# Four graph layers on one core: the last stage's weights and the split of their products made in the graph layer, flags and rows turned by transposes, the first unit's projection split by VectorE

## The chip, the cores and the metric

The kernel runs on one core of a Trainium2 chip. A core has TensorE (PE, with its weight loads shown apart as PEld), VectorE (DVE), ScalarE (ACT), GpSimd (POOL), and SyncE (SP), which here issues the DMA transfers. The metric is the time of one execution on the device in microseconds, as the median of several runs; lower is better.

## The reference

Four residual layers over x of shape [8, 1024, 64] (batch, node, feature) with one adjacency matrix adj [1024, 1024] of zeros and ones. Before each there is a layer norm and a relu:

```python
h = maximum(layernorm(x), 0); x = x + hypergraph_layer(h, ...)      # L0
h = maximum(layernorm(x), 0); x = x + graph_attention(h, adj, ...)  # L1
h = maximum(layernorm(x), 0); x = x + graph_layer(h, adj, ...)      # L2
h = maximum(layernorm(x), 0); x = x + last_attention(h, adj, ...)   # L3

def graph_layer(x, A, weights):          # two rounds
    for i in range(2):
        x = relu(einsum('bmf,fg->bmg', einsum('mn,bnf->bmf', A, x), weights[i]))

def gat_layer(x, graph, W, b):           # used by last_attention
    h = x @ W                            # per head 64 -> 128; at the end 1024 -> 64
    s = einsum('bnd,bmd->bnm', h, h) * graph
    s = where(s == 0.0, -1e16, s)
    return einsum('bnm,bmd->bnd', softmax(s, axis=2), h) + b

def last_attention(x):                   # 8 heads, then one more attention over their outputs
    heads = [gat_layer(x, graph, Wh[i], bh[i]) for i in range(8)]
    x = leaky_relu(concat(heads), 0.01)
    return leaky_relu(gat_layer(x, graph, W_out, b_out), 0.01)
```

## The kernel before

The four layers run one after the other as four stages; x, h and the adjacency stay on the core between them. The change touches the third stage (graph layer, function `graph_layer`) and the fourth (`last_attention`).

**The graph layer** goes through quarters of two batches: rows are turned, projected with a weight (L880 for the second), parted into a rounded high and a low float32r half, and multiplied with the adjacency. The second product, L905, is the last large one; behind each of its eight tiles DVE adds x (L1065) and the layer norm for the next stage follows. At its end the stage makes what the next one needs of rows that are all zero: flags `gl_zero` [128, 8] for each of eight tiles become the rows `marks` [8, 1024] by eight fp32 matmuls against the identity (L939), and counts [8, 1024] become columns by eight more (L945). DVE's L1139 makes `row_scale` of them.

**The last stage** works in units. A head unit is one batch and one head; there are 64, in order of batches, and then eight output units, one per batch. As h W Wᵀ hᵀ is wanted, the kernel forms the gram matrix W Wᵀ of each head once (W stacked twice, so 128 x 128), splits it into high and low halves, and projects y = gram · rows (`project`, L303). Of a unit:

- PE's `project` writes y for unit g+2; ACT rounds it to `y_hi` (`round_y`, L519) and copies it to `y_wide` (`copy_y`, L526); POOL subtracts and adds the marks, giving `y_lo` (`split_y`, L637 and L639).
- For each of eight tiles of 128 rows PE makes four matmuls of 512 columns (`score`, L318: rows `hid_xs` against y high and low), DVE masks the tile with the adjacency and takes the row maximum (`mask_tile`, L450), ACT takes the exponential (L535), DVE transposes the tile in 32 x 32 blocks (`turn_tile`, L459). Scores run two tiles ahead of DVE, in two PSUM buffers.
- Four parts of 32 small matmuls (`values`, L338) then sum the values of the unit before, and `head_out`, `project_out` carry it on.

The rows `hid_xs` of a batch are its h turned by `turn_rows(n, part, bank)`: for each of four tiles two fp32 matmuls of h (128 x 64) against the identity, one written to PSUM partitions 0 to 63, one to 64 to 127 (L282). ACT rounds them (`round_rows`, L512), DVE subtracts in the upper half (`split_rows`, L421), so that the upper half holds the low part. For batches 1 to 7 the two parts are turned behind tile 6 of the units 3 and 4 of the batch before (units are counted from 0), between that tile's scores and `project_out`. Output units call `turn_rows` for both parts in `project`.

**Order.** No planner is at work: each engine's program is the order written in the loops over g and t, and engines wait for each other by counting semaphores. At the start of the last stage the order on PE is: turn both parts for batch 0, wait for the weights, eight gram matmuls (in each round ACT takes the high half, DVE the low half, L484, before PSUM is free again), `project(0)`, `project(1)`, `score(0)`. On SP: the marks to DRAM (L230), six weight loads (L232), x saved to DRAM (L233), the marks read back to all partitions (L227), then the rows that `values` wants. The weights land in `weights_t`, a buffer that the first `turn_tile` overwrites later. L43 is a line of the start of a stage's block.

Of the kernel before, what the change touches and what calls it, by code (L numbers as in the profile page):

```python
# [5 lines left out]
ALU = mybir.AluOpType  # L6
# [6 lines left out]
P = 128  # L13
B, N, F = 8, 1024, 64
NT = N // P
# [34 lines left out]
def split(nc, ctx, name, shape):  # L50

    return (ctx.enter_context(nc.sbuf_tensor(name + "_hi", shape, F32R)),
            ctx.enter_context(nc.sbuf_tensor(name + "_lo", shape, F32R)))


def last_attention(nc, m, w, d, x_saved):
# [9 lines left out]
    with ExitStack() as ctx:  # L66
# [6 lines left out]
        wh_t, wz, wo, bias, weights_t = w.wh_t, w.wz, w.wo, w.bias, w.weights_t  # L73
        gram = split(nc, ctx, name + "_gram", [P, HEADS, P])
# [30 lines left out]
        gram_ready = sem("gram_ready")  # L105
        gram_hi = sem("gram_hi")
        gram_split = sem("gram_split")
# [3 lines left out]
        weights_loaded = sem("weights_loaded")  # L111
# [66 lines left out]
        def _(sp):  # L178
# [52 lines left out]
            for place, src in w.loads:  # L231
                sp.dma_start(place, src).then_inc(weights_loaded, 16)  # L232
# [44 lines left out]
        def _(pe):  # L277
            def turn_rows(n, part, bank):
                for k in range(4):
                    t = 4 * part + k  # L280
                    for c in range(2):
                        ins = pe.matmul(m.ps_low[c * F:(c + 1) * F, bank, k * P:(k + 1) * P],  # L282
                                        m.h[:, t, n, :], m.ident[:], start=True, stop=True)
                return ins
# [132 lines left out]
        def _(dve):  # L417
# [91 lines left out]
        def _(act):  # L509
# [2103 lines left out]
```

## Time and profile before

| | us |
|---|---|
| median of 3 runs | 2303.24 (2299.11 to 2304.76) |
| profiled execution, its own time | 2298.83 |
| span in the profile | 2296.8 |
| PE busy | 2048.7 (89%) |
| DVE busy | 2022.9 (88%) |
| ACT busy | 1406.3 (61%) |
| POOL busy | 950.3 (41%) |
| PEld busy | 1352.5 (59%) |

The profile is of one execution. The span is the time from the first to the last recorded instruction; the execution's own time is 2.0 us longer. Busy shares are means over four stages that work differently: the last stage begins at 742 us and has two thirds of the span. In a timeline row the number ahead is the start in us, the next the length; an "x32" joins 32 records of one kind, and the bracket gives the idle time of the engine just before and what ended it. fp32 matmuls have two records each.

### The profile page before, as it was taken

How to read it: one execution, taken by the hardware profiler on the slowest of the kernel's cores; microseconds unless marked ns; L12 is line 12 of the kernel's file. 1: busy time of each engine (PE TensorE's matmuls, PEld its weight loads, DVE VectorE, ACT ScalarE, POOL GpSimd, SP SyncE). 2: the span in 40 equal slices, each digit the busy share in tenths (PEclk: the TensorE clock that was granted, in tenths of full speed). 3: DMA queues.
4: the chain of work that ended last, by engine and by line, in shares of the span. 5: the costliest groups of instructions: out<-in, count | busy, mean ns of one | idle time of the engine just before them, and what ended most of it. 6: DMA issues, size and time to landing. Idle time of an engine off the chain costs nothing. (4 is left out here: it accounts for less than half of the span.)

```text
span 2296.8 us, 61374 instructions
## 1 busy us (share of the span) xinstructions
PE 2048.7 (89%) x26446; PEld 1352.5 (59%) x26446; DVE 2022.9 (88%) x2704; ACT 1406.3 (61%) x2186; POOL 950.3 (41%) x542
## 2 busy tenths in 40 slices
PE   5888867478688699999999999999999999998886
PEld 5654436345476466666666666666666666665555
DVE  7568857499657699999999999999999999999995
ACT  4422225499631467666777666776667676676774
POOL 2259972136400244444444344444444444432211
PEclk9999977578988799999999999999999999999998
DMA  3000000534200320021111211201210210123442
GB/s 127 1 0 0 0 1 1 93 65 67 38 2 11 92 53 30 29 57 39 41 42 33 53 34 39 53 25 39 52 43 30 57 30 30 34 58 65 71 66 47
DMA packets 176817, 94.72 MB, mean 41 GB/s; under 512 B 158552, under 2 KB 163864, under 8 KB 176432
## 3 DMA queue, kind: packets, MB, share of 16 engines
q1 hardware_dynamic: 176560, 90.94, 18.0%
q8 instruction: 204, 3.34, 0.6%
q14 instruction: 53, 0.43, 0.1%
HBM read 80.09 MB, written 10.83 MB: 40 GB/s over the span
## 5 line engine op out<-in xcount | busy, mean ns | idle before, releaser
L535 ACT ACTIVATE x_sb<-x_sb,hid_neg_max 128x1024 f32<-128x1024 f32 x576 | 661.6, 1154 | 289.6 <-DVE hid_neg_max L450 289.4
L459 DVE STREAM_TRANSPOSE hid_weights_t<-x_sb 128x1024 f32<-128x1024 f32 x576 | 709.2, 1231 | 1.6 <-ACT x_sb L535 1.2
L450 DVE CUSTOM_DVE_ANT_0 x_sb<-ps_score,adj_mask,row_scale 128x1024 f32<-128x1024 f32 x512 | 636.1, 1242 | 16.2 <-PE ps_score L318 15.0
L338 PE MATMUL ps_low<-hid_weights_t,hid_x_rep 32*64 32x256 f32 x18432 | 577.5, 384 | 11.1 <-ACT hid_share L565 10.7
L318 PE MATMUL ps_score<-hid_y_hi,hid_xs 128*128 128x512 f32 x1152 | 522.7, 454 | 33.0 <-DVE hid_neg_max L450 27.4
L338 PEld LDWEIGHTS ps_low<-hid_weights_t,hid_x_rep 32*64 32x64 f32 x18432 | 393.2, 132 | 169.4 <-issue 98.0
L318 PE MATMUL ps_score<-hid_y_lo,hid_xs 128*128 128x512 f32 x1152 | 457.1, 397 | 0.0
L645 POOL TENSOR_TENSOR hid_z<-hid_z,hid_inv_cols 128x1024 f32<-128x1024 f32 x64 | 194.1, 3032 | 554.6 <-ACT hid_z L543 554.6
L318 PEld LDWEIGHTS ps_score<-hid_y_hi,hid_xs 128*128 128x128 f32 x1152 | 217.6, 189 | 259.7 <-issue 155.2
L318 PEld LDWEIGHTS ps_score<-hid_y_lo,hid_xs 128*128 128x128 f32 x1152 | 218.9, 190 | 44.2 <-issue 15.0
L637 POOL TENSOR_TENSOR hid_y_wide<-hid_y_wide,hid_y_hi 128x1024 f32<-128x1024 f32 x64 | 153.5, 2398 | 192.0 <-ACT hid_y_wide L526 192.0
L639 POOL TENSOR_TENSOR hid_y_lo<-hid_y_wide,marks 128x1024 fp32r<-128x1024 f32 x64 | 152.9, 2389 | 5.0
L350 PE MATMUL ps_low<-hid_z,hid_wz 128*128 128x512 f32 x256 | 121.8, 598 | 4.4 <-DVE hid_xs L421 3.9
L535 ACT ACTIVATION_READ_ACCUMULATOR x_sb<-x_sb,hid_neg_max 128x1 f32 x576 | 112.1, 195 | 0.0
L543 ACT COPY hid_z<-ps_low 128x1024 f32<-128x1024 f32 x72 | 73.1, 1016 | 47.7 <-PE ps_low L338 47.7
L2157 POOL TENSOR_TENSOR h_sb<-h_sb,hyp_share 128x512 f32<-128x512 f32 x72 | 94.9, 1318 | 5.7
L519 ACT CAST hid_y_hi<-ps_low 128x1024 fp32r<-128x1024 f32 x72 | 73.1, 1015 | 29.0 <-PE ps_low L303 16.5
L1397 ACT ACTIVATE ps_score<-gat_e_wide,e 128x1024 f32<-128x1024 f32 x64 | 70.8, 1107 | 25.0 <-PE ps_score L1272 19.1
L578 ACT COPY hid_share<-ps_low 128x512 f32<-128x512 f32 x56 | 32.9, 588 | 81.9 <-PE ps_low L366 81.9
L656 POOL TENSOR_TENSOR h_sb<-h_sb,hid_share 128x512 f32<-128x512 f32 x56 | 74.5, 1330 | 17.2 <-ACT hid_share L578 17.2
L2139 ACT ACTIVATE hyp_blend_exp<-ps_score,hyp_minus_one 128x512 f32<-128x512 f32 x54 | 37.1, 688 | 71.3 <-PE ps_score L2120 71.3
L450 DVE CUSTOM_DVE_ANT_0 x_sb<-ps_score,hid_masks,hid_row_flag 128x1024 f32<-128x1024 f32 x64 | 79.3, 1239 | 0.0
(349 smaller groups left out, 3059.9 us busy)
## 6 DMA issues: line engine op xcount, KB each, us to landing
hid_inv_cols<-hid_inv_rows SPq DMA_DIRECT2D x64, 512.0 KB, 3.7
hid_x_rep<-hid_row_space SPq DMA_DIRECT2D x64, 256.0 KB, 5.7
gat_x_rep<-gat_row_space SPq DMA_DIRECT2D x32, 256.0 KB, 5.7
gat_e_wide<-gat_e_space SPq DMA_DIRECT2D x8, 512.0 KB, 6.4
marks<-hid_mark_rows SPq DMA_DIRECT2D x8, 512.0 KB, 5.0
x_sb<-in_x SPq DMA_DIRECT2D x4, 512.0 KB, 6.0
hyp_neighbours<-in_adj SPq DMA_DIRECT2D x4, 512.0 KB, 7.2
edge_adj_high<-in_adj SPq DMA_DIRECT2D x4, 512.0 KB, 8.9
```

The costliest lines, as they stand in the source:

```text
L318: ins = pe.matmul(m.ps_score[:, i % 2, half * HALF:(half + 1) * HALF], xs[:, batch_of(g) % 2, t * P:(t + 1) * P], y[g % 2][k][:, half * HA ...
L338: ins = pe.matmul(m.ps_low[c * F:(c + 1) * F, a, 0:NT * Q], x_rep[a * Q:(a + 1) * Q, batch_of(g) % 2, b, :], weights_t[a * Q:(a + 1) * Q, ...
L350: ins = pe.matmul(m.ps_low[:, half, :], wz[:, g % HEADS, :], z[:, half * HALF:(half + 1) * HALF], start=True, stop=True)
L450: dve.tensor_tensor_reduce(ring[:, i % RING, :], m.ps_score[:, i % 2, :], mask, scale, HUGE, ALU.add, ALU.min, neg_max[:, g % 2, t:t + 1]) ...
L459: dve.transpose(weights_t[:, g % 2, :, t, :], ring[:, i % RING, :].rearrange("p (b j) -> p b j", j=Q)).then_inc(tile_turned, 1)
L519: act.copy(y[g % 2][0][:], wide(y_banks(g))).then_inc(y_hi, 1)
L535: act.activation(ring[:, i % RING, :], ring[:, i % RING, :], ACT.Exp, scale=-1.0, bias=neg_max[:, g % 2, t:t + 1], accum_out=row_sum[:, g ...
L637: pool.tensor_tensor(y_wide[:], y_wide[:], y[g % 2][0][:], ALU.subtract).then_inc(y_lo, 1)
L639: pool.tensor_tensor(y[g % 2][1][:], y_wide[:], m.marks[:], ALU.add).then_inc(y_split, 1)
L645: pool.tensor_tensor(rows, rows, inv_cols[:].rearrange("p i t -> p t i"), ALU.mult)\
L656: pool.tensor_tensor(out, out, share[:].rearrange("p (t f) -> p t f", f=F), ALU.add)\
L2157: pool.tensor_tensor(rows[:, t, :], rows[:, t, :], s, ALU.add)\
```

## The change

- `last_weights` is called ahead of `graph_layer`; the six weight loads are issued on SP in the graph layer, behind that layer's own four. `wh_t` and the gram get buffers of their own, on the other side of SBUF ("right").
- The eight gram matmuls stand in the graph layer as `square_weights`, between the last projection and the second product, into one PSUM bank pair; ACT copies the high half and DVE takes the low half in one instruction each.
- Flags and counts are turned by `pe.transpose` in place of matmuls with the identity.
- In `turn_rows` the lower half is made by `pe.transpose`, the upper half stays a matmul. Output units and head units use the same function.
- The first unit's `copy_y` (ACT) and `split_y` (POOL, two operations) are gone; DVE makes both from PSUM, behind `split_rows`.

```diff
@@ last_attention, SP
             sp.dma_start(mark_rows, m.marks[0:B, :]).then_inc(marks_stored, 16)
-            for place, src in w.loads:
-                sp.dma_start(place, src).then_inc(weights_loaded, 16)
             sp.dma_start(x_saved, m.x[:].rearrange("p t b f -> p (t b f)")).then_inc(x_copied, 16)
@@ last_attention, PE
             def turn_rows(n, part, bank):
                 for k in range(4):
                     t = 4 * part + k
-                    for c in range(2):
-                        ins = pe.matmul(m.ps_low[c * F:(c + 1) * F, bank, k * P:(k + 1) * P],
-                                        m.h[:, t, n, :], m.ident[:], start=True, stop=True)
+                    pe.transpose(m.ps_low[0:F, bank, k * P:(k + 1) * P], m.h[:, t, n, :], m.ident[:])
+                    ins = pe.matmul(m.ps_low[F:P, bank, k * P:(k + 1) * P], m.h[:, t, n, :], m.ident[:],
+                                    start=True, stop=True)
                 return ins
...
             for part in range(2):
                 turn_rows(0, part, prep_bank(0, part)).then_inc(x_turned, 1)
-            pe.wait_ge(weights_loaded, 16 * len(w.loads))
             pe.wait_ge(x_split, 2)
-            for h in range(HEADS):
-                if h > 1:
-                    pe.wait_ge(gram_split, h - 1)
-                w2 = wh_t[:, h, :, :].rearrange("p a f -> p (a f)")
-                pe.matmul(m.ps_low[:, h % 2, 0:P], w2, w2, start=True, stop=True).then_inc(gram_ready, 1)
-            pe.wait_ge(gram_split, HEADS)
             project(0)
@@ last_attention, DVE
             split_rows(0, 1)
-            for h in range(HEADS):
-                dve.wait_ge(gram_hi, h + 1)
-                dve.tensor_tensor(gram[1][:, h, :], m.ps_low[:, h % 2, 0:P], gram[0][:, h, :],
-                                  ALU.subtract).then_inc(gram_split, 1)
+            dve.wait_ge(y_hi, 1)
+            dve.tensor_tensor(y_wide[:], wide(y_banks(0)), y[0][0][:], ALU.subtract).then_inc(y_copied, 1)
+            dve.wait_ge(y_copied, 1)
+            dve.wait_ge(marks_loaded, 16)
+            dve.tensor_tensor(y[0][1][:], y_wide[:], m.marks[:], ALU.add).then_inc(y_split, 1)
             dve.wait_ge(x_copied, 16)
@@ last_attention, ACT
-            for h in range(HEADS):
-                act.wait_ge(gram_ready, h + 1)
-                act.copy(gram[0][:, h, :], m.ps_low[:, h % 2, 0:P]).then_inc(gram_hi, 1)
             round_y(0)
-            copy_y(0)
             round_y(1)
@@ last_attention, POOL
-            split_y(0)
@@ graph_layer, SP
+            for place, src in last.loads:
+                sp.dma_start(place, src).then_inc(last_loaded, 16)
@@ graph_layer, PE
+            def square_weights():
+                pe.wait_ge(last_loaded, 16 * len(last.loads))
+                pe.wait_ge(parted[0], 2 * QB)
+                for h in range(HEADS):
+                    w2 = last.wh_t[:, h, :, :].rearrange("p a f -> p (a f)")
+                    ins = pe.matmul(m.ps_score[:, 1, h * P:(h + 1) * P], w2, w2, start=True, stop=True)
+                ins.then_inc(gram_ready, 1)
...
             project_second(QB - 1)
+            square_weights()
...
             pe.wait_ge(flags_ready, 1)
+            pe.wait_ge(gram_split, 1)
             for t in range(NT):
-                ins = pe.matmul(m.ps_score[0:B, 1, t * P:(t + 1) * P], zero[:, t, :], m.ident[:],
-                                start=True, stop=True)
+                ins = pe.transpose(m.ps_score[0:B, 1, t * P:(t + 1) * P], zero[:, t, :], m.ident[:])
...
             for t in range(NT):
-                ins = pe.matmul(m.ps_low[:, 0, t * B:(t + 1) * B], counts[:, t * P:(t + 1) * P],
-                                m.ident[0:B, 0:B], start=True, stop=True)
+                ins = pe.transpose(m.ps_low[:, 0, t * B:(t + 1) * B], counts[:, t * P:(t + 1) * P],
+                                   m.ident[0:B, 0:B])
@@ graph_layer, ACT, behind the last round_second
+            act.wait_ge(gram_ready, 1)
+            act.copy(last.gram[0][:].rearrange("p h c -> p (h c)"), m.ps_score[:, 1, :]).then_inc(gram_hi, 1)
@@ graph_layer, DVE, behind the last part_second
+            dve.wait_ge(gram_hi, 1)
+            gram_lo = last.gram[1][:].rearrange("p h c -> p (h c)")
+            dve.tensor_tensor(gram_lo, m.ps_score[:, 1, :], last.gram[0][:].rearrange("p h c -> p (h c)"),
+                              ALU.subtract).then_inc(gram_split, 1)
```

PE's order at the start of the last stage, from the counts' last matmuls to the first projection. `h_sb` are the rows to be turned. Before:

```order
L945 MATMUL ps_low<-ident,gl_counts 128x8 x8
L782 UNCONDITIONAL_BRANCH
L276 UNCONDITIONAL_BRANCH
L282 MATMUL ps_low<-ident,h_sb 64x128 x16
L379 MATMUL ps_low<-hid_weights_t 128x128 x8
L303 MATMUL ps_low<-hid_xs,hid_gram_hi 128x512
```

After, where L275 is the transpose and L276 the matmul (the pair stands eight times):

```order
L940 MATMUL ps_low<-ident,gl_counts 128x8 x8
L764 UNCONDITIONAL_BRANCH
L270 UNCONDITIONAL_BRANCH
L275 MATMUL ps_low<-ident,h_sb 64x128
L276 MATMUL ps_low<-ident,h_sb 64x128
L275 MATMUL ps_low<-ident,h_sb 64x128
L276 MATMUL ps_low<-ident,h_sb 64x128
```

The same sixteen instructions turn the rows, now of two kinds in turn, and the eight gram matmuls between them and the projection are gone.

They stand in the graph layer now, between the last projection and the second product. PE there, before:

```order
L880 MATMUL ps_score<-gl_w,gl_bent 128x128 x16
L905 MATMUL ps_low<-gl_second_hi,adj_t_sb 128x512
L905 MATMUL ps_low<-gl_second_lo,adj_t_sb 128x512
L905 MATMUL ps_low<-gl_second_hi,adj_t_sb 128x512
```

After:

```order
L874 MATMUL ps_score<-gl_w,gl_bent 128x128 x16
L841 MATMUL ps_score<-hid_wh_t 128x128 x8
L899 MATMUL ps_low<-gl_second_hi,adj_t_sb 128x512
L899 MATMUL ps_low<-gl_second_lo,adj_t_sb 128x512
```

The second product starts behind eight instructions more.

DVE's order at the start of the last stage, from the last operation of the graph layer to the first mask (written ISA). Before:

```order
L1139 SCALAR_TENSOR_TENSOR row_scale<-ps_low,gl_sign 128x64
L782 UNCONDITIONAL_BRANCH
L416 UNCONDITIONAL_BRANCH
L421 TENSOR_TENSOR hid_xs<-ps_low,hid_xs 64x512 x2
L484 TENSOR_TENSOR hid_gram_lo<-ps_low,hid_gram_hi 128x128 x8
L450 ISA x_sb,hid_neg_max<-ps_score,adj_mask,row_scale 128x1024
```

After:

```order
L1140 SCALAR_TENSOR_TENSOR row_scale<-ps_low,gl_sign 128x64
L764 UNCONDITIONAL_BRANCH
L403 UNCONDITIONAL_BRANCH
L408 TENSOR_TENSOR hid_xs<-ps_low,hid_xs 64x512 x2
L470 TENSOR_TENSOR hid_y_wide<-ps_low,hid_y_hi 128x1024
L473 TENSOR_TENSOR hid_y_lo<-hid_y_wide,marks 128x1024
L437 ISA x_sb,hid_neg_max<-ps_score,adj_mask,row_scale 128x1024
```

Eight small subtractions are replaced by two operations of 1024 columns, the second of which reads the marks.

## Rows read from the trace of the kernel before

**Rows 1.** Stretch, its length, busy PE, PEld, DVE, ACT, POOL, clock, DMA share, GB/s
```profile
742.40:769.10 26.70, 14.54 (x61) 11.30 (x62) 3.72 (x10) 7.42 (x14) 5.00 (x3) 0.56 0.90 200
769.10:2063.00 1293.90, 1274.80 (x19264) 822.01 (x19271) 1286.82 (x1678) 896.82 (x1358) 577.35 (x263) 1.00 0.16 40
2063.00:2296.80 233.80, 189.30 (x2980) 130.76 (x2962) 208.67 (x258) 158.07 (x311) 49.99 (x31) 0.92 0.36 61
```

**Rows 2.** Timeline (start, length, engine, line, operation, idle before), start of last stage
```profile
742.44 3.68 PE L282 MATMUL ps_low<-ident,h_sb 128*64 128x128 f32 x32 [1.16 <-PEq L43]
...
746.16 0.59 ACT L512 CAST hid_xs<-ps_low 128x512 fp32r<-128x512 f32 x1 [1.12 <-PE ps_low L282]
...
746.78 0.69 DVE L421 TENSOR_TENSOR hid_xs<-ps_low,hid_xs 64x512 fp32r<-64x512 f32 x1 [1.01 <-ACT hid_xs L512]
748.06 0.43 SPq L233 DMA_DIRECT2D x_saved<-x_sb  x1
...
751.66 1.22 PE L379 MATMUL ps_low<-hid_weights_t 128*128 128x128 f32 x4 [5.53 <-DMA hid_bias<-in_bh_t]
...
757.99 0.79 PE L303 MATMUL ps_low<-hid_xs,hid_gram_hi 128*128 128x512 f32 x1 [0.68 <-DVE hid_gram_lo L484]
...
760.10 1.01 ACT L519 CAST hid_y_hi<-ps_low 128x1024 fp32r<-128x1024 f32 x1 [2.49 <-PE ps_low L303]
...
766.92 0.79 PE L318 MATMUL ps_score<-hid_y_hi,hid_xs 128*128 128x512 f32 x1 [5.15 <-POOL hid_y_lo L639]
...
769.15 1.28 DVE L450 CUSTOM_DVE_ANT_0 x_sb<-ps_score,adj_mask,row_scale 128x1024 f32<-128x1024 f32 x1 [11.21 <-PE ps_score L318]
```

**Rows 3.** DMA issue there: count, KB, us from issue to landing
```profile
marks<-hid_mark_rows SPq DMA_DIRECT2D x1, 512.0 KB, 10.6
```

**Rows 4.** Timeline, PE between the last projection and the second product
```profile
690.25 2.02 PE L880 MATMUL ps_score<-gl_w,gl_bent 128*128 128x128 f32 x16 [1.45 <-issue]
...
692.78 0.50 PE L905 MATMUL ps_low<-gl_second_hi,adj_t_sb 128*128 128x512 f32 x1 [0.51 <-DVE gl_second_lo L1052]
```

**Rows 5.** Timeline, DVE at the second product's second tile
```profile
700.39 0.69 DVE L1065 SCALAR_TENSOR_TENSOR x_sb<-ps_low,x_sb 128x512 f32<-128x512 f32 x1 [0.36 <-PE ps_low L905]
```

**Rows 6.** Timeline of the end of the graph layer
```profile
734.19 3.58 PE L939 MATMUL ps_score<-ident,gl_zero 128*8 128x128 f32 x16 [0.71 <-DVE gl_zero L1132]
...
737.70 3.58 PE L945 MATMUL ps_low<-ident,gl_counts 8*128 8x8 f32 x16
...
741.32 0.23 DVE L1139 SCALAR_TENSOR_TENSOR row_scale<-ps_low,gl_sign 128x64 f32<-128x64 f32 x1 [2.30 <-PE ps_low L945]
```

**Rows 7.** Timeline, PE around one output unit's turned rows
```profile
2092.67 0.40 PE L318 MATMUL ps_score<-hid_y_hi,hid_xs 128*128 128x512 f32 x1
2092.91 0.40 PE L318 MATMUL ps_score<-hid_y_lo,hid_xs 128*128 128x512 f32 x1
2093.23 1.97 PE L282 MATMUL ps_low<-ident,h_sb 128*64 128x128 f32 x32
2095.13 0.50 PE L318 MATMUL ps_score<-hid_y_hi,hid_xs 128*128 128x512 f32 x1
2095.47 0.40 PE L318 MATMUL ps_score<-hid_y_lo,hid_xs 128*128 128x512 f32 x1
```

**Rows 8.** The weight loads of these turned rows
```profile
2093.23 1.73 PEld L282 LDWEIGHTS ps_low<-ident,h_sb 128*64 128x64 f32 x32 [0.37 <-issue]
```

**Rows 9.** Timeline, PE and PEld: eight transposes, 64 columns wide
```profile
95.71 1.00 PEld L1971 LDWEIGHTS ps_score<-ident,table_elus 128*64 128x64 f32 x8
...
95.94 1.04 PE L1971 MATMUL ps_score<-ident,table_elus 128*64 128x128 f32 x8
...
96.90 0.29 PEld L1975 LDWEIGHTS ps_score<-hyp_rank,hyp_upper 64*128 64x128 f32 x2 [0.20 <-issue]
```

**Rows 10.** Timeline, DVE behind a head unit's turned rows
```profile
1031.46 1.28 DVE L450 CUSTOM_DVE_ANT_0 x_sb<-ps_score,adj_mask,row_scale 128x1024 f32<-128x1024 f32 x1 [0.23 <-PE ps_score L318]
```

**Rows 11.** DVE's waits, last stage to 2063: us in total, times, longest
```profile
DVE x_sb L450 <- PE ps_score L318: 15.0, 17, 11.2
```

More of the change, by code:

```diff
@@ L47, with split @@
     pass
-def split(nc, ctx, name, shape):
-    return (ctx.enter_context(nc.sbuf_tensor(name + "_hi", shape, F32R)),
-            ctx.enter_context(nc.sbuf_tensor(name + "_lo", shape, F32R)))
+def split(nc, ctx, name, shape, side="left"):
+    return (ctx.enter_context(nc.sbuf_tensor(name + "_hi", shape, F32R, side=side)),
+            ctx.enter_context(nc.sbuf_tensor(name + "_lo", shape, F32R, side=side)))
 def last_attention(nc, m, w, d, x_saved):
@@ L71, in sem @@
             return nc.alloc_semaphore(f"{name}_{n}")
-        wh_t, wz, wo, bias, weights_t = w.wh_t, w.wz, w.wo, w.bias, w.weights_t
-        gram = split(nc, ctx, name + "_gram", [P, HEADS, P])
+        wz, wo, bias, gram = w.wz, w.wo, w.bias, w.gram
+        weights_t = sb("weights_t", [P, 2, NB, NT, Q])
         ring = m.x[:].rearrange("p (r t) b f -> p r (t b f)", r=RING)
@@ L103, in last_attention @@
         col_rows = nc.dram_tensor("hid_col_rows", (B, P, NT), BF16).ap()
-        gram_ready = sem("gram_ready")
-        gram_hi = sem("gram_hi")
-        gram_split = sem("gram_split")
         x_copied = sem("x_copied")
@@ L110, in last_attention @@
         out_rows_loaded = sem("out_rows_loaded")
-        weights_loaded = sem("weights_loaded")
         rows_saved = sem("rows_saved")
@@ L637, in split_y @@
                 pool.tensor_tensor(y_wide[:], y_wide[:], y[g % 2][0][:], ALU.subtract).then_inc(y_lo, 1)
-                pool.wait_ge(y_lo, g + 1)
+                pool.wait_ge(y_lo, g)
                 pool.tensor_tensor(y[g % 2][1][:], y_wide[:], m.marks[:], ALU.add).then_inc(y_split, 1)
@@ L700, with __init__ @@
 class Weights:
-    def __init__(self, nc, ctx, name):
-        self.nc, self.ctx, self.name, self.clear, self.loads = nc, ctx, name, [], []
+    def __init__(self, nc, ctx, name, side="left"):
+        self.nc, self.ctx, self.name, self.clear, self.loads, self.side = nc, ctx, name, [], [], side
     def buffer(self, n, shape):
-        return self.ctx.enter_context(self.nc.sbuf_tensor(f"{self.name}_{n}", shape, F32))
+        return self.ctx.enter_context(self.nc.sbuf_tensor(f"{self.name}_{n}", shape, F32, side=self.side))
     def load(self, place, src):
@@ L758, in graph_weights, with last_weights @@
     return g
-def last_weights(nc, ctx, d):
-    g = Weights(nc, ctx, "hid")
-    g.weights_t = g.buffer("weights_t", [P, 2, N // 32, NT, 32])
-    g.wh_t = g.weights_t[:, 0, 0:4, :, :].rearrange("p a (h k) i -> p (a h) (k i)", k=4)\
-        .rearrange("p h (k f) -> p h k f", k=2)
+def last_weights(nc, ctx, own, d):
+    g = Weights(nc, ctx, "hid", "right")
+    g.wh_t = own.enter_context(nc.sbuf_tensor("hid_wh_t", [P, HEADS, 2, F], F32))
+    g.gram = split(nc, ctx, "hid_gram", [P, HEADS, P], "right")
     g.wz = g.buffer("wz", [P, HEADS, HID])
@@ L774, in last_weights, with graph_layer @@
     return g
-def graph_layer(nc, m, g):
+def graph_layer(nc, m, g, last):
     QB = B // 2
@@ L810, in graph_layer @@
         mixed, mix_bent = sem("mixed"), sem("mix_bent")
+        last_loaded, gram_ready, gram_hi, gram_split = (
+            sem("last_loaded"), sem("gram_ready"), sem("gram_hi"), sem("gram_split"))
         summed, x_added = sem("summed"), sem("x_added")
@@ L2564, in four_layers @@
             with fresh_semaphores(nc), ExitStack() as own:
-                graph_layer(nc, m, graph_weights(nc, own, d))
-        with fresh_semaphores(nc), ExitStack() as own:
-            g = last_weights(nc, own, d)
+                g = last_weights(nc, ctx, own, d)
+                graph_layer(nc, m, graph_weights(nc, own, d), g)
+        with fresh_semaphores(nc):
             x_saved = nc.dram_tensor("x_saved", (P, NT * B * F), F32).ap()
```

## The prediction

> **What bounds the kernel now.** Read the page first for the shares: DVE is busy 88% and PE 89% of the span. That is an average, so read the busy time by stage next [rows 1]. In the 64 head units (769.1 to 2063) DVE is busy 1286.8 of 1293.9 us, PE 1274.8: DVE sets the pace and PE stands just behind. The waits say how close: DVE waited for a score tile 17 times, 15.0 us in all, and 11.2 of that is the one wait before its first tile [rows 11, 2]. So 16 small waits, 3.8 us, are left, and the timeline shows where they sit, for example 0.23 us right behind a unit's turned rows [rows 10]. I counted them in DVE's timeline: nearly all follow a turn of rows. Whatever lengthens PE there is paid by DVE; in units without a turn PE has a few tenths to spare.
>
> The other place is the start of the last stage, 742.4 to 769.1, where DVE works 3.7 of 26.7 us [rows 1]. Read it as a chain in the timeline [rows 2]: rows turned on PE from 742.44, taken by ACT at 746.16 and by DVE until 747.47, then PE idle for the last weight transfer until 751.66, eight rounds of PE, ACT and DVE for the gram until 757.99, projection until 760.10, rounding on ACT, two subtractions and additions on POOL, first scores at 766.92, DVE's first tile at 769.15.
>
> **The change, part by part.** All times are of the profiled execution (span 2296.8, its own time 2298.83 us); the median of the runs is 2303.24. I carry differences over to the median.
>
> *Flags and counts by transposes.* Each of the 16 fp32 matmuls there is two records: 16 records from 734.19 to 737.70, and 16 more, 3.58 us, to the end at 741.32 [rows 6]. A transpose is one record per tile: eight of them pass in 1.04 us elsewhere in the kernel [rows 9], (1.04 - 0.27)/7 = 0.11 us each, 0.27 being the last one's own length. So half the records go: 3.51/2 + 3.58/2, less a little tail, is 3.4 us gained. Between nothing (a transpose as long as two records) and 3.5. On the path, since DVE's last operation waits for it. The marks' DVE operation fits beside the counts' transposes.
>
> *Gram in the graph layer.* Eight matmuls, 16 records like those of the projection before them. That projection starts at 690.25 and its slots are over at about 690.25 + 2.02 - 0.16 = 692.1; 16 more at 0.11 make 1.75, so the second product starts at 693.9 instead of 692.78 [rows 4]: 1.1 us late. DVE is the slower engine in that product but starts on PE's tiles, and waits 0.36 us for the second [rows 5], so all of it is paid. ACT's copy (1.01, as the rounding in rows 2) and DVE's subtraction (1.28, as L450 there) fall into the idle stretch before DVE's first tile at about 697.9: 693.9 + 0.3 + 1.0 + 1.3 = 696.5. Nothing. Bounds for the matmuls: 0.6 (partly beside the wait that is there) to 2.9 (at the half clock). The weights' six transfers run over 60 us before they are used.
>
> So the last stage starts 3.4 - 1.1 = 2.3 us sooner, at about 740.1.
>
> *Start of the last stage.* The wait for weights and the gram rounds are gone. POOL's two operations become two of DVE, 1.28 each. From the end of the turning to DVE's first tile: 746.16 to 747.47 (1.31), 0.1, projection 757.99 to 760.10 (2.11), rounding 1.01, DVE 2 x 1.28, small hand-overs 0.1, then 766.92 to 769.15 (2.23): 9.4 us. What is late next: the marks, which the second DVE operation needs. They landed 748.54 + 10.6 = 759.1, that is 11.1 us behind the issue of x_saved, their predecessor in the queue [rows 2, 3]. x_saved is now issued behind one small transfer at 740.4, so the marks are there at 751.5 at the latest, earlier by up to 2 us since no weights are ahead. Were turning as long as before (3.72 us), DVE would be ready for the marks at 740.1 + 3.72 + 9.4 - 2.23 - 1.28 = 749.7, would wait for them, and the first tile would stand at 755.0: 14.2 us gained, 15.9 without the wait.
>
> *Turned rows: the term that goes the other way.* Per tile two matmuls of 64 columns turn the same rows into the lower and the upper 64 partitions. Now they run side by side: 32 records take 1.90 us from 2093.23 to 2095.13, 0.22 us per pair of matmuls less the switch, where two records one behind the other take 0.22 by themselves [rows 7]. The lower one becomes a transpose. Three rows speak on whether it still shares the array. The scores before the turned rows pass every 0.24 us (2092.67, 2092.91), but the first turned row starts 0.32 behind, its weights loaded only then, PEld idle 0.37 [rows 7, 8]: entering the side-by-side form costs 0.09, with its exposed load 0.14. Leaving it costs 0.09, and the next record follows at 0.34 instead of 0.24: another 0.10, for 128 columns of weights; for 64 I take half. The 64-column transposes there are [rows 9] behave otherwise: their first weights load while the full-width matmul streams and no gap opens, and the matmul after them waits, PEld idle 0.20. So a transpose of this form looks like an operation of the full array, and alternating with a half-width matmul means two switches per tile. Per tile: transpose 0.11, into it 0.14, matmul 0.22, into that 0.14: 0.61 against 0.22. A part of four tiles: 0.11 + 4 x 0.36 + 3 x 0.25 = 2.3 against 0.14 + 0.88 = 1.0, 1.3 us more. Bounds: nothing (side by side as before) to 1.8 (if each switch also bares the 128-column load).
> The Trainium skill says the same from the other side: the page TensorEngine Tiling (Array Packing), Restrictions and Gotchas, Gotcha 2, has column tiling and transposes of fp32 exclude each other on trn2. No row here shows the two alternate. By the rule the sum is the one below; without it the first rival's.
>
> Seven batches turn two parts each inside head units, and there PE's lateness is DVE's wait [rows 10]: 14 x 1.3 = 18.2, less about 0.07 each where PE still had something in hand: 17.2 us lost. At the start of the stage, at the half clock (0.56 over that stretch [rows 1]), a pair takes 3.72/8 = 0.46; records double, switches perhaps not: 0.9 to 1.2 per tile, eight tiles, 3.5 to 6 us more, I take 4.5. The marks hide 1.8 of it: 14.2 becomes 11.5. In the last eight units eight tiles are turned per unit, 2.7 us more on PE, but PE is busy 189.3 of 233.8 us there [rows 1] and DVE's tiles take longer than PE's; I take 0.5 in all.
>
> Sum: -11.5 + 17.2 + 0.5 = +6.2 us. Profiled 2305.0; as a median 2309.4. About 0.3% (6.9 us) is what a measurement of this kernel tells from no change, so this is the edge of it, 0.27%. The case itself spans +1 to +13.
>
> **Rivals.** *The transpose shares the array.* Then only the start counts: -14.2 to -15.9, 2288. For it: the two matmuls share today. Against: the loads that hide [rows 9]. The Trainium skill's page Perfetto Trace Analysis, section Transposes, asks for transposes in place of matmuls, as cheaper; the trace agrees [rows 9] for a run of them alone.
> *One behind the other, without switches.* 0.11 per tile more, 0.43 per part: 14 x 0.43 - 0.9 = 5.1; at the start 1.7, hidden by the marks. -14.2 + 5.1 = -9.1: 2294. Against it: both switches in rows 7.
> *Slower: the cover in the last eight units fails.* The turning stands between two score tiles: 2.7 us more make it 4.6, with the tiles' scores 6.5, while DVE has two tiles in hand, about 5.2. Each of eight units loses 1.3, 10 us more: 2320. It decides once PE's burst is longer than DVE's two tiles. Against: PE idles a fifth of that stretch.
>
> **How the numbers follow.** Main case 0.5; shared array 0.1; one behind the other 0.2; failed cover 0.13; the rest (marks or clock otherwise) 0.07. Faster by over 0.3% is the shared case, most of the serial one and little else: 0.28. Within: a bit over half of the main case and edges: 0.34. Slower: 0.38. Range: leave out the shared case and the far end: 2291 to 2319. The main case by itself: 2304 to 2316.
>
> **What would show it.** The stage's first DVE tile near 757.6 (755 if transposes share); transposes and matmuls of the turned rows starting 0.2 to 0.4 us apart in turn, not together; a part of 2.3 us; DVE waits of 1.3 to 1.5 us in the fourth and fifth unit of every batch, some 20 us in all; L905 1.1 us later; the flags' two groups half as long. I am wrong if a part still takes 1.0 us, or if DVE does not wait behind it.

## The result and the profile after

The changed kernel takes 2317.69 us in the median (2316.77 to 2318.48, 4 runs), the kernel before 2302.25 (2299.11 to 2304.76, 4 runs with those shown above): a ratio of 1.0069, 95% interval 1.0057 to 1.0081. It is 15.4 us slower. The forecast was 2309.4: the direction is the forecast one, but two terms of the sum were too small. The measured time lies inside the stated range (2291 to 2319) and outside the main case's (2304 to 2316).

The profiled execution has a span of 2315.0 us, 18.2 more than before. Not all of it belongs to the change. The first two stages are the same code in both, and yet DVE's first reduction of the graph layer stands at 633.14 instead of 629.49; over all profiled kernels it lay between 628.5 and 637.2. So I count from that instruction:

| us | before | after |
|---|---|---|
| graph layer, to `row_scale` | 111.8 | 108.8 |
| to the last stage's first tile on DVE | 139.7 | 127.1 |
| from there to the end of the first unit | 24.8 | 25.7 |
| 56 units more | 1137.8 | 1156.9 |
| 8 units more | 173.3 | 174.0 |
| rest (the last seven output units and what follows them) | 191.9 | 198.2 |
| from the graph layer to the end | 1667.4 | 1681.9 |

(A unit's end is DVE's reciprocal of its row sums, one row per unit in the timeline. The 56 units hold all fourteen turned parts of head units; the eight behind them are seven head units and the first output unit.) Three terms stand out: -12.6 at the start, +19.2 in the head units, +6.3 in the output units.

The same windows by stage as in [rows 1], of after:

```profile
743.02:760.21 17.19, 13.84 (x37) 7.65 (x38) 3.84 (x5) 4.48 (x5) 0.32 (x1) 0.50 0.96 230
760.21:2078.00 1317.79, 1300.04 (x19218) 830.26 (x19217) 1288.45 (x1678) 897.60 (x1359) 577.86 (x263) 1.00 0.16 40
2078.00:2315.00 237.00, 201.55 (x2892) 133.33 (x2890) 198.91 (x257) 157.14 (x309) 50.66 (x31) 0.93 0.36 60
```

In the head units DVE is as busy as before (1288.5 against 1286.8 us), while the 56 units of the table are 19.2 us longer. DVE's waits say why; of after, from the first tile to 2078 (us in total, times, longest), to be laid beside [rows 11]:

```profile
DVE x_sb L437 <- PE ps_score L312: 29.1, 26, 2.8
```

Of these, 2.3 are the wait of the first tile, which in [rows 11] was 11.2. So where there were 16 small waits with 3.8 us there are 25 now with 26.8. Fourteen of them stand one each behind the fourteen turned parts of the head units; they last 1.43 to 1.61 us each, 21.3 in all. The timeline of PE and DVE there, of after, where L275 is the transpose and L276 the matmul:

```profile
858.58 0.40 PE L312 MATMUL ps_score<-hid_y_lo,hid_xs 128*128 128x512 f32 x1
859.02 0.30 PE L275 MATMUL ps_low<-ident,h_sb 128*64 128x128 f32 x1
859.25 0.43 PE L276 MATMUL ps_low<-ident,h_sb 128*64 128x128 f32 x2
859.62 0.30 PE L275 MATMUL ps_low<-ident,h_sb 128*64 128x128 f32 x1
859.85 0.43 PE L276 MATMUL ps_low<-ident,h_sb 128*64 128x128 f32 x2
...
862.25 0.50 PE L312 MATMUL ps_score<-hid_y_hi,hid_xs 128*128 128x512 f32 x1
...
863.49 1.28 DVE L437 CUSTOM_DVE_ANT_0 x_sb<-ps_score,adj_mask,row_scale 128x1024 f32<-128x1024 f32 x1 [1.61 <-PE ps_score L312]
```

A pair starts every 0.60 us: 0.23 from the transpose to the matmul, 0.37 from the matmul with its two records to the next transpose. The forecast had 0.61 (0.25 and 0.36). DVE waits 1.61 us behind it, where before it waited 0.23 behind such a part [rows 10].

The start of the last stage, of after, beside [rows 2]:

```profile
743.05 0.40 PE L275 MATMUL ps_low<-ident,h_sb 128*64 128x128 f32 x1 [1.36 <-PEq L43]
...
750.19 0.69 PE L276 MATMUL ps_low<-ident,h_sb 128*64 128x128 f32 x2
750.92 0.59 ACT L500 CAST hid_xs<-ps_low 128x512 fp32r<-128x512 f32 x1 [3.31 <-PE ps_low L276]
...
752.28 0.80 PE L297 MATMUL ps_low<-hid_xs,hid_gram_hi 128*128 128x512 f32 x1 [1.40 <-DVE hid_xs L408]
...
755.44 1.22 DVE L470 TENSOR_TENSOR hid_y_wide<-ps_low,hid_y_hi 128x1024 f32<-128x1024 f32 x1 [3.21 <-ACT hid_y_hi L507]
...
756.70 1.22 DVE L473 TENSOR_TENSOR hid_y_lo<-hid_y_wide,marks 128x1024 fp32r<-128x1024 f32 x1
...
760.21 1.28 DVE L437 CUSTOM_DVE_ANT_0 x_sb<-ps_score,adj_mask,row_scale 128x1024 f32<-128x1024 f32 x1 [2.28 <-PE ps_score L312]
```

Turning takes 7.8 us instead of 3.7, and still the stage's first tile comes 17.2 us behind its first turned row instead of 26.7. The wait for weights and the rounds of the gram are gone, and no wait for the marks is seen: they had landed (issued 744.91, 7.4 us) when DVE came to them.

The flags, and the gram in the graph layer, of after:

```profile
695.77 1.95 PE L841 MATMUL ps_score<-hid_wh_t 128*128 128x128 f32 x16
...
697.48 0.47 PE L899 MATMUL ps_low<-gl_second_hi,adj_t_sb 128*128 128x512 f32 x1
...
738.88 1.87 PE L935 MATMUL ps_score<-ident,gl_zero 128*8 128x128 f32 x8 [0.71 <-DVE gl_zero L1133]
...
740.68 1.02 PE L940 MATMUL ps_low<-ident,gl_counts 8*128 8x8 f32 x8
...
741.93 0.20 DVE L1140 SCALAR_TENSOR_TENSOR row_scale<-ps_low,gl_sign 128x64 f32<-128x64 f32 x1
```

The second product starts 64.3 us into the graph layer (697.48 - 633.14) instead of 63.3 (692.78 - 629.49, [rows 4]): 1.05 us for the gram. The two groups of [rows 6] take 1.87 and 1.02 us instead of 3.58 each.

In the output units another engine shows the cost. ACT around the turned rows of an output unit, of after (L507 rounds them, L523 is the exponential), and DVE's next block transpose:

```profile
2135.97 1.02 ACT L507 CAST hid_y_hi<-ps_low 128x1024 fp32r<-128x1024 f32 x1 [4.22 <-PE ps_low L276]
...
2137.79 1.15 ACT L523 ACTIVATE x_sb<-x_sb,hid_neg_max 128x1024 f32<-128x1024 f32 x1
...
2142.98 1.19 ACT L523 ACTIVATE x_sb<-x_sb,hid_neg_max 128x1024 f32<-128x1024 f32 x1
...
2144.30 1.25 DVE L446 STREAM_TRANSPOSE hid_weights_t<-x_sb 128x1024 f32<-128x1024 f32 x1 [1.83 <-ACT x_sb L523]
```

The tile whose mask was over at 2132.3 could have had its exponential at once. It got it at 2137.79: ACT's program has the rounding of the turned rows ahead of it, and ACT stood waiting for them for 4.22 us. The work that piled up on ACT also made the next tile's exponential late (2142.98), and that is the one DVE waits for. Over the stretch ACT's waits for them were, of before and then of after:

```profile
ACT hid_y_hi L519 <- PE ps_low L282: 11.2, 7, 1.9
```

```profile
ACT hid_y_hi L507 <- PE ps_low L276: 30.0, 7, 4.6
```

DVE, which before had no wait for scores or exponentials over 0.15 us from 2063 on, has 13.6 us of them from 2078 on in after: 8.6 for exponentials, 5.0 for scores. The loss of 6.3 us in the table's rest is less than half of that, because something else got shorter at the same time: 25 of DVE's mask operations (L435 before, L422 after) stand in that stretch, and they take 37.8 us before and 30.8 after. The last section shows what they depend on.

### The profile page after: what moved, and what is told of

Read it like the earlier page. It is cut to its first block and busy times, and to the rows that moved or that the text cites. A ratio compares the mean times of both kernels' runs of the same rounds, so it can differ in the third digit from the quotient of the medians.

```text
span 2315.0 us, 61072 instructions
## 1 busy us (share of the span) xinstructions
PE 2089.7 (90%) x26302; PEld 1364.1 (59%) x26302; DVE 2016.4 (87%) x2699; ACT 1404.2 (61%) x2178; POOL 946.7 (41%) x540
## 5 line engine op out<-in xcount | busy, mean ns | idle before, releaser
L523 ACT ACTIVATE x_sb<-x_sb,hid_neg_max 128x1024 f32<-128x1024 f32 x576 | 661.5, 1153 | 266.7 <-DVE hid_neg_max L437 266.5
L523 ACT ACTIVATION_READ_ACCUMULATOR x_sb<-x_sb,hid_neg_max 128x1 f32 x576 | 112.0, 195 | 0.0
L507 ACT CAST hid_y_hi<-ps_low 128x1024 fp32r<-128x1024 f32 x72 | 73.1, 1015 | 54.0 <-PE ps_low L276 34.0
```

The lines of the kernel that those rows point to most:

```text
L507: act.copy(y[g % 2][0][:], wide(y_banks(g))).then_inc(y_hi, 1)
L523: act.activation(ring[:, i % RING, :], ring[:, i % RING, :], ACT.Exp, scale=-1.0, bias=neg_max[:, g % 2, t:t + 1], accum_out=row_sum[:, g ...
```

## Experiments

One theory and its rivals were left after the two traces. *A*: the loss is the alternation of a transpose with a half-width matmul, in the head units by PE alone, in the output units by way of ACT's order. The rivals: the loss has another source (buffers moved to the other side of SBUF, or PE's idle time at the start gone), or needs the rest of the change; and for the output units, PE's burst alone starves DVE. All times of stages are counted as in the table above: first tile / 56 units / rest / all from the graph layer on.

| | median us | ratio to before | first tile | 56 units | rest | all |
|---|---|---|---|---|---|---|
| before | | 1 | 139.7 | 1137.8 | 191.9 | 1667.4 |
| after | 2317.7 | 1.0069 (1.0057 to 1.0081) | 127.1 | 1156.9 | 198.2 | 1681.9 |
| turn_matmul | 2287.4 | 0.9929 (0.9910 to 0.9948) | 123.2 | 1138.3 | 193.2 | 1653.4 |
| before_turned | 2326.9 | 1.0106 (1.0086 to 1.0126) | 139.9 | 1156.5 | 199.0 | 1694.9 |
| turn_grouped | 2293.5 | 0.9962 (0.9946 to 0.9977) | 122.2 | 1146.0 | 191.0 | 1657.6 |
| act_order | 2305.8 | 1.0029 (1.0020 to 1.0038) | 126.2 | 1156.9 | 190.0 | 1671.2 |
| act_order_matmul | 2278.5 | 0.9899 (0.9884 to 0.9914) | 122.1 | 1138.1 | 188.6 | 1644.5 |
| flags_matmul | 2288.8 | 0.9943 (0.9928 to 0.9958) | 126.4 | 1138.2 | 193.2 | 1656.7 |
| pool_split | 2291.2 | 0.9954 (0.9939 to 0.9969) | 126.2 | 1138.3 | 191.8 | 1654.5 |
| best | 2280.6 | 0.9903 (0.9887 to 0.9920) | 121.9 | 1138.2 | 188.6 | 1645.1 |
| marks_first | 2282.8 (1 run) | | 121.9 | 1138.2 | 191.8 | 1650.0 |
| gram_late | 2287.8 (1 run) | | 127.1 | 1138.1 | 192.3 | 1655.9 |

The kernel before, run beside each group: 2301.3 (turn_matmul to turn_grouped), 2299.6 (act_order to pool_split), 2303.9 (the last three). Where a stage is compared to a us, the traces decide, since the two stages ahead move the whole by several us from one execution to the next. But each trace is one execution too. Kernels with the same code up to that point differ in the first tile by 1.1 us (turn_matmul 123.2, act_order_matmul 122.1) and by 0.9 (after 127.1, act_order 126.2); those with the same output units differ in the rest by 1.4 (191.8 to 193.2). The 56 units repeat to 0.2 (1138.1 to 1138.3). A difference of about 1 us outside the 56 units is therefore not shown by one pair of traces.

**turn_matmul**: undo one part.

```diff
-                    pe.transpose(m.ps_low[0:F, bank, k * P:(k + 1) * P], m.h[:, t, n, :], m.ident[:])
-                    ins = pe.matmul(m.ps_low[F:P, bank, k * P:(k + 1) * P], m.h[:, t, n, :], m.ident[:],
-                                    start=True, stop=True)
+                    for c in range(2):
+                        ins = pe.matmul(m.ps_low[c * F:(c + 1) * F, bank, k * P:(k + 1) * P],
+                                        m.h[:, t, n, :], m.ident[:], start=True, stop=True)
```

> The changed kernel, but all rows are turned by the two half-width matmuls again. Theory (the transposes of turned rows cost; all other parts of the change gain): the fourteen turned parts in head units give back 14 x 1.37 = 19 us, the output units some 7, the start of the last stage 4 (turning 3.7 us instead of 7.8), in all about -30 against the changed kernel: 2288, and about 15 us faster than the kernel before. Rival (the loss has another cause, as the buffers moved to the other side of SBUF or the missing idle time): at most 10 us come back, 2308 or more.

2287.4 us, faster than before by 0.7%. The 56 units are back at 1138.3, the first tile comes 3.9 us sooner, the rest is 5.0 shorter. The loss is the turned rows'; the rival falls. At the start the shorter turning (4.1 us) is not the only thing that moved. DVE now waits 1.2 us for the marks, while the projection runs faster: from its first matmul to ACT's rounding it takes 1.24 us here, at a granted clock of 1.00, against 2.12 us in after, at 0.50.

**before_turned**: the same three lines the other way round, in the kernel before.

> The kernel before, with the lower half of every turned row made by a transpose and nothing else changed. Theory: +19 us in the head units, +7 in the output units, nothing at the start (PE waits for the last weights until 751.7 there, and the turning, 7.8 us instead of 3.7, is over by then): 2302 + 26 = 2328. Rival (the loss needs the other parts of the change): under +10, 2312 or less. On the output units alone: if the loss there is from ACT waiting for the rows, it is +5 to +9 here too; if it is an accident of how masks and GpSimd met, it is between 0 and +14.

2326.9: +18.7 in the 56 units, +7.1 in the rest, +0.2 at the first tile. The loss needs nothing else of the change, and at the start the weights hid it.

**turn_grouped**: the switch against the load.

```diff
                 for k in range(4):
                     t = 4 * part + k
                     pe.transpose(m.ps_low[0:F, bank, k * P:(k + 1) * P], m.h[:, t, n, :], m.ident[:])
+                for k in range(4):
+                    t = 4 * part + k
                     ins = pe.matmul(m.ps_low[F:P, bank, k * P:(k + 1) * P], m.h[:, t, n, :], m.ident[:],
```

> The changed kernel, but of each part first the four transposes and then the four half-width matmuls. The pairs now start every 0.60 us. Theory A (each switch between a transpose and a half-width matmul costs 0.12 to 0.14): only two switches are left of eight, a part takes 4 x 0.11 + 0.13 + 4 x 0.22 + 0.13 = 1.6 us instead of 2.3: 0.75 x 14 = 10 us less in the head units, 4 in the output units, 3 at the start (half clock): 2300. Theory B (every load of 64 columns is bare, whatever the record ahead was): a part still takes 2.3 us, the time stays within 2 us of 2317.7. Theory C (the transposes then hide beside the matmuls): 2290 or less.

The 56 units gain 10.9 us, as theory A had it; the start gains 4.9 and the rest 7.1, more than was put down. At the start the expectation reckoned with the half clock, and 0.66 was granted over this run's turning (747 to 752), 0.50 over that of after (743 to 751). B is out, and C too, since 8 us are still missing against two matmuls. A part in turn_grouped (L275 transposes, L278 matmuls, L362 the output projection):

```profile
834.73 0.63 PE L275 MATMUL ps_low<-ident,h_sb 128*64 128x128 f32 x4
835.28 0.76 PE L278 MATMUL ps_low<-ident,h_sb 128*64 128x128 f32 x5
835.78 0.64 PE L362 MATMUL ps_low<-hid_hidden,hid_wo 128*64 128x512 f32 x1
835.88 0.49 PE L278 MATMUL ps_low<-ident,h_sb 128*64 128x128 f32 x3
...
837.16 0.50 PE L314 MATMUL ps_score<-hid_y_hi,hid_xs 128*128 128x512 f32 x1
```

Four transposes pass in 0.55 us with one switch behind them. The first matmul of the output projection, which goes to the other half, starts while the last matmuls of the upper half still come: half-width matmuls share, and here the transposes did not. In turn_matmul the sharing is plain, since the records of the two halves start in twos, the first at 854.53 and 854.54 and from the second two on a new one about every 0.11 us:

```profile
854.53 1.09 PE L276 MATMUL ps_low<-ident,h_sb 128*64 128x128 f32 x16
855.46 1.03 PE L360 MATMUL ps_low<-hid_hidden,hid_wo 128*64 128x512 f32 x4
856.42 0.50 PE L312 MATMUL ps_score<-hid_y_hi,hid_xs 128*128 128x512 f32 x1
```

From the first turned row to the next score: 1.89 us here, 2.43 in groups, 3.23 in turn, the same for all fourteen parts of each run. The differences to turn_matmul, 1.34 in turn and 0.54 in groups, times 14 parts are 18.8 and 7.6; the 56 units lost 18.6 and 7.7 against turn_matmul.

**act_order**: the changed kernel, ScalarE's order alone.

```diff
                     if g < UNITS:
                         exp_tile(g * NT + t)
+                    if t == 0 and HEAD_UNITS <= g + 1 < UNITS:
+                        round_y(g + 1)
...
-                    if t == 7 and g + 2 < UNITS:
+                    if t == 7 and g + 2 < HEAD_UNITS:
                         round_y(g + 2)
```

> The changed kernel, but for output units ScalarE rounds the turned rows (round_y) behind the next unit's first exponential instead of ahead of it. In the changed kernel ScalarE waits 30.0 us there in seven waits (11.2 before), with that exponential queued behind it. Theory (the output units lose their 6 to 7 us because ScalarE's queue stands behind the longer turning): DVE's waits for the exponential there, 8.6 us in all, go, and the part behind the 65th unit's start takes 190 to 193 us instead of 198.2; the whole 2317.7 - 6 = 2312. Rival (PE's burst of 4.7 us starves DVE of scores by itself): it stays at 197 or more, 2317.

The rest falls from 198.2 to 190.0 us with PE's burst as long as before. ACT waits 17.3 us for the rows instead of 30.0, and DVE's waits from 2077 on, of act_order, are:

```profile
DVE hid_weights_t L446 <- ACT x_sb L523: 5.0, 5, 1.1
DVE x_sb L437 <- PE ps_score L312: 1.3, 2, 0.7
```

They were 8.6 and 5.0 in after. The mask operations of the rest take the same time in both (30.9 and 30.8 us), so the 8.2 us are mostly these 7.3 us of waits. The theory named the size of the gain, but not its parts: the waits for exponentials were to go, and 5.0 us of them stay, while the waits for scores, which it did not name, fell by 3.7. So ACT's order makes somewhat more than half of what DVE waits in the output units, and the rival, a burst of PE that starves DVE by itself, is wrong for most of it. The cause of the 6.3 us that stay is not separated. Only part of the 11.9 us between the medians is the edit's: in the traces 1.8 us of the gain stand at the first tile and in the first unit, which it does not touch.

**act_order_matmul**: both edits together.

> The same move on ScalarE, with all rows turned by matmuls. There ScalarE waits only about 11 us for the rows. Theory: DVE is busy 90% of the output units there, so little is left to gain: 1 to 3 us less than with the matmuls alone, 2285. Rival (ScalarE's later rounding delays the next unit's rows): 0 to 4 us more, 2290.

2278.5 us, 1.0% faster than before, the lowest of all. The move gains more than I put down: 4.6 us in the rest and 2.4 in the eight units ahead of it (170.7 instead of 173.1), against turn_matmul. But not by way of DVE's waits for exponentials, of which there were none to speak of in turn_matmul's output units. The traces show where it comes from. In the rest the mask operations are 2.8 us shorter (34.7 instead of 37.5), and the stretch behind DVE's last instruction is 1.8 shorter (24.5 instead of 26.3), a stretch that took 24.9 to 26.3 in the five kernels with turn_matmul's output units, so this part may be chance. In the eight units ahead the masks are 1.4 shorter and DVE's small waits 1.0. One such mask operation beside GpSimd's, of turn_matmul and then of act_order_matmul:

```profile
2139.60 2.37 POOL L616 TENSOR_TENSOR hid_y_lo<-hid_y_wide,hid_y_hi 128x1024 fp32r<-128x1024 f32 x1 [19.07 <-ACT hid_y_wide L514]
2140.42 2.63 DVE L422 TENSOR_TENSOR hid_masks<-adj_mask,hid_col_mask 128x2048 bf16<-128x2048 bf16 x1
```

```profile
2133.92 2.38 POOL L618 TENSOR_TENSOR hid_y_lo<-hid_y_wide,hid_y_hi 128x1024 fp32r<-128x1024 f32 x1 [18.22 <-ACT hid_y_wide L514]
2135.56 1.81 DVE L422 TENSOR_TENSOR hid_masks<-adj_mask,hid_col_mask 128x2048 bf16<-128x2048 bf16 x1
```

The new order lets ACT's copy, and with it GpSimd's operation, come 0.8 us sooner against the mask, which then has less of it to sit out. It is so in five of the last six units with such a meeting; in one (2161.12) the mask starts 0.4 us behind GpSimd and takes 3.09 us.

**flags_matmul**: on turn_matmul, `pe.transpose` of flags and counts back to `pe.matmul` with start and stop.

> Rows turned by matmuls, and flags and counts turned by matmuls too. Counted from the start of the graph layer, row_scale is made at +108.8 us with transposes. Theory (16 records less, 3.1 us between the kernels and 1.05 for the gram that came in): +112.9, the first tile of the last stage 4.1 later, and the time 2287.4 + 4 = 2291.5. Rival (a transpose is paid like two records; the gain is from elsewhere): within 1 us of 108.8.

`row_scale` at +111.5, so the transposes gain 2.7, and 3.2 at the first tile. It is less than 4.1 because the counts' matmuls had the higher clock in this run (0.65 granted over 737 to 743, where before had 0.50 over both groups):

```profile
737.17 3.58 PE L935 MATMUL ps_score<-ident,gl_zero 128*8 128x128 f32 x16 [0.71 <-DVE gl_zero L1134]
...
740.68 2.18 PE L941 MATMUL ps_low<-ident,gl_counts 8*128 8x8 f32 x16
```

The first group takes 3.58 as in [rows 6], the second 2.18 instead of 3.58. What raised the clock here and not before stays open. The medians do not separate this kernel from turn_matmul (1.4 us apart, intervals that overlap).

**pool_split**: on turn_matmul, DVE's two operations out, `copy_y(0)` and `split_y(0)` back.

> Rows turned by matmuls, and the first unit's y split by ScalarE's copy and GpSimd again. Theory: from the end of the rounding to the first score 5.8 us as before, against 3.8 now of which 1.2 is a wait for the marks: the first tile 2.0 us later, 2289.4. Rival (the marks or DVE's place in the chain hide it): less than 0.5 us.

The first tile is 3.0 us later, not 2.0. POOL waits for the marks ahead of its first operation, where DVE waits only ahead of its second; so on POOL both operations stand behind the marks:

```profile
756.13 2.34 POOL L617 TENSOR_TENSOR hid_y_wide<-hid_y_wide,hid_y_hi 128x1024 f32<-128x1024 f32 x1 [9.31 <-DMA marks<-hid_mark_rows]
758.54 2.34 POOL L619 TENSOR_TENSOR hid_y_lo<-hid_y_wide,marks 128x1024 fp32r<-128x1024 f32 x1
```

So the 3.0 us are the price of this order as much as of the engine. The medians are 3.8 us apart in the same direction, with intervals that overlap.

**marks_first** and **best**: the marks' transfer ahead of the saving of x, on turn_matmul and on act_order_matmul.

```diff
-            sp.dma_start(x_saved, m.x[:].rearrange("p t b f -> p (t b f)")).then_inc(x_copied, 16)
             sp.wait_ge(marks_stored, 16)
             load_marks(0)
+            sp.dma_start(x_saved, m.x[:].rearrange("p t b f -> p (t b f)")).then_inc(x_copied, 16)
```

> Rows turned by matmuls, and the marks read back ahead of the saving of x; ScalarE's order as in the changed kernel. Theory as for the kernel before this one: first tile at +122.0 instead of +123.2. Rival: +124 to +125, a wait for the saved x ahead of the first tile.

> Rows turned by matmuls, ScalarE's rounding behind the next exponential in output units, and the marks read back ahead of the saving of x. With the rows turned by matmuls the first unit's second DVE operation waits 1.2 us for the marks. Theory (their transfer stands behind the 2 MB of x): it lands 2 to 4 us sooner, the first tile stands at +121 us from the start of the graph layer instead of +122.1 to +123.2, and the time is about 2277.5. Rival (DVE's first tile then waits for x to be saved, which is issued 2 us later and takes 7.5): +123 or more, 2280.

The marks land in 4.3 us instead of 7.8, and their wait, 1.18 us in turn_matmul, is gone. Another takes its place; DVE's first tile in turn_matmul and in marks_first:

```profile
757.07 1.28 DVE L437 CUSTOM_DVE_ANT_0 x_sb<-ps_score,adj_mask,row_scale 128x1024 f32<-128x1024 f32 x1 [2.28 <-PE ps_score L312]
```

```profile
753.04 1.28 DVE L437 CUSTOM_DVE_ANT_0 x_sb<-ps_score,adj_mask,row_scale 128x1024 f32<-128x1024 f32 x1 [2.27 <-DMA x_saved<-x_sb]
```

The tile overwrites x and waits for its copy. The first tile came 1.2 us sooner in marks_first (121.9 against 123.2) and 0.2 sooner in best (121.9 against 122.1). As the two kernels without the edit are 1.1 apart themselves, no gain of the edit is shown. The medians of best and act_order_matmul, 2280.6 and 2278.5, ran beside different executions of before, and their ratios can't be told apart.

**gram_late**: on turn_matmul, loads in the graph layer, but the eight gram rounds in the last stage again (`z` lies over the weights' buffer there).

> Rows turned by matmuls, weights loaded in the graph layer, but the gram made in the last stage again in eight rounds. Theory: the second product starts 1.0 us sooner, the eight rounds take 6.2 us in the chain, 1.2 us of which the wait for the marks hides: the first tile at +123.2 - 1.0 + 6.2 - 1.2 = +127.2. Rival (the rounds hide beside the wait for the marks): +124 or less.

First tile at +127.1, 3.9 us behind turn_matmul's, as the sum had it. Its terms came out less well, and it is chance that their errors cancel: the rounds take 5.7 us (743.80 to 749.53) and not 6.2, the projection to ACT's rounding takes 2.1 us instead of turn_matmul's 1.24, and the first tile follows the first score after 1.7 us instead of 2.23.

## Why the prediction was right or wrong

- *What bounds the kernel.* Right: PE's lateness behind turned rows became DVE's wait, part for part. Of the 15 small waits that stand behind a turn of rows before, though, seven stand behind rows that the change leaves alone (L290).
- *Flags and counts*: 3.4 forecast. Between the two kernels 4.1 (3.05 sooner in spite of 1.05 for the gram), since the second group, 8 x 8 each, went from 3.58 to 1.02 us and not to half. By flags_matmul it is 2.7 to `row_scale` and 3.2 to the first tile; the 1.4 us that the first of these lacks to 4.1 are the higher clock of that run's second group.
- *Gram in the graph layer*: 1.1 forecast, 1.05 measured, and DVE carried it unchanged from the first tile of the product (+68.3 against +67.3) to the last (+100.0 against +99.0).
- *Start of the last stage*: -11.5 forecast to the first tile, -12.6 measured. Turning was 3.5 to 6 us longer by the forecast, and is 4.1. The marks were to hide 1.8 of it; with the turning short they cost 1.2 us, with it long nothing. What the forecast did not have is the clock of the projection behind the turning, 1.24 us against 2.12 (turn_matmul), which offsets most of the marks' wait: 3.9 us are left of the 4.1.
- *Turned rows*: the step that decided the sign. That a transpose of this form does not share the array, with two switches per tile, was read from three rows of before and holds to 0.02 us per pair. By the rule cited there from the Trainium skill, TensorEngine Tiling (Array Packing), Restrictions and Gotchas, Gotcha 2, fp32 transposes and column tiling exclude each other; turn_grouped and turn_matmul agree with it, 2.43 against 1.89 us. 17.2 forecast, 19.2 measured. The term was mis-sized by the slack of 0.07 us per part that I took off and by 0.04 in the part itself: DVE had no slack left, it lost 1.37 per part, and PE 1.34. My own rows said so, as DVE already waited 0.23 us in [rows 10], behind a part whose rows were turned the short way.
- *Output units*: 0.5 forecast; 6.3 between the two kernels, 5.0 and 7.1 by the turned rows alone (turn_matmul, before_turned). This step failed. I argued from PE's idle fifth and from the tiles in hand of DVE, and named a rival in which PE's burst is longer than these. I never asked who is queued behind the instruction that waits for the turned rows. ACT's rounding waits, and the next exponential is behind it. act_order shows it for 7.3 of the 13.6 us that DVE waits; the 6.3 that stay, 5.0 of them for exponentials, are open.
- *The sum*: +6.2 forecast; +14.5 from the graph layer on, +15.4 in the medians. Of the 8.3 missing (14.5 - 6.2), 5.8 are the output units and 2.0 the head units; 0.9 behind the first tile and 0.8 behind the 57th unit were not forecast, and 1.1 more was gained at the start. That the median fell into the range is in part luck: DVE's waits in the output units were longer than the whole loss there, and 7.0 us came back in mask operations that met less of GpSimd's work, which I had not foreseen either. With them as long as before the time would have been near 2325 (an estimate, 2317.7 + 7.0), above the range.
- *Chances*: the serial case without switches had 0.2 and is refuted by the 0.60 us per pair; the shared array had 0.1 and is refuted by the rows of after, where transposes and matmuls start in turn, and by turn_grouped. The failed cover had 0.13 and 10 us; DVE did lack scores in the output units, for 5.0 us, but act_order took most of that away with PE's burst as long as before.

## What to carry to other kernels

Two half-width matmuls that write different halves ran at the price of one here; making one of them a transpose ended that and added two switches per pair, so turn either both ways with matmuls or, where transposes are wanted, in a run of their own. When a step on one engine gets longer, follow not only the engine that reads the result but everything queued behind its wait. And when a wait at a stage's start is removed, count what hid behind it: here the longer turning cost nothing in before_turned at that place, and 3.9 us in after. Before the gain of a new order is put down to the wait it was meant to remove, look whether that wait was there at all; in act_order_matmul it was not.

## What the runs showed of the hardware

- A pair of a 64-column transpose and a half-width fp32 matmul: 0.60 us, against 0.23 for two half-width matmuls side by side (four pairs in 0.93 us in turn_matmul), 0.22 for a half-width matmul alone (two records 0.11 apart, turn_grouped from 835.28) and 0.11 for a transpose in a run, all at a granted clock of 1.00.
- DVE's bf16 mask operation (L435, L422) takes 1.22 us, but up to 3.1 where it starts while GpSimd is at work. Of before, at 2126.25 it takes 2.62, with GpSimd busy from 2125.42 for 2.37 us, and so ends 1.08 us behind GpSimd. All nine long ones of before start inside a GpSimd operation and end 1.08 us behind it, as if they had stood still for it. The f32 operation ahead of this one takes 1.25 beside the same GpSimd operation.

```profile
2125.07 1.25 DVE L450 CUSTOM_DVE_ANT_0 x_sb<-ps_score,hid_masks,hid_row_flag 128x1024 f32<-128x1024 f32 x1
...
2126.25 2.62 DVE L435 TENSOR_TENSOR hid_masks<-adj_mask,hid_col_mask 128x2048 bf16<-128x2048 bf16 x1
```

```profile
2125.42 2.37 POOL L632 TENSOR_TENSOR hid_y_lo<-hid_y_wide,hid_y_hi 128x1024 fp32r<-128x1024 f32 x1 [5.29 <-ACT hid_y_wide L526]
```

  The 32 of them take 50.0 us before and 40.1 after, 40.0 in before_turned and 49.3 in turn_matmul: it is the longer turning that moved them off GpSimd's operations. It so gave 9.9 us of DVE time back, 7.0 of them in the last seven output units, which hides part of what it cost there.
- The two unchanged stages ahead take between 628.5 and 637.2 us to the graph layer's first reduction in the profiled executions. A difference of a few us between single executions says nothing of a change unless it is traced to the place where the change acts.
